# Second layer: the memory's four products by ScalarE with a per-partition scale, in place of two VectorE products

## The reference, cut to what matters

```python
q = x @ Wq.T; k = x @ Wk.T; v = x @ Wv.T            # q: 4 queries x 8 heads x 16, k and v: 8 heads x 16
a_dot   = softmax(q k / 4) v                         # 32 heads of 16
sigma_q = elu(q)                                     # four blocks of 128 features
a_mem   = sigma_q @ memory / (sigma_q @ memory_norm) # one divisor for each token and block
w       = sigmoid(memory_weight)
out     = a_dot * (1 - w) + a_mem * w
```

## Time and profile before

| | |
|---|---|
| median of three runs | 4788.65 us |
| the profiled execution's own time | 4785.47 us |
| its span, first to last instruction | 4783.7 us |
| mean granted TensorE clock | 0.98 of full speed |
| TensorE busy | 4368.3 us (91%) |
| VectorE busy | 3613.1 us (76%) |
| ScalarE busy | 2432.1 us (51%) |
| row maxima on VectorE, L2055, 2048 of them | 1270.6 us busy, 682 ns each |
| exponentials on ScalarE, L1489, 2048 of them | 1090.9 us busy, 602 ns each |
| memory products on VectorE, L2035, 128 of them | 411 to 426 ns each, median 419 |

### The profile page before, as it was taken

How to read it: one execution, slowest core, us unless ns; L and a number is a source line. 1 busy time by engine, 2 the same in 40 slices (tenths; PEclk the granted TensorE clock), 3 DMA queues, 4 the chain that set the end, 5 groups by cost and what they waited for, 6 DMA issues and landing times.

```text
span 4783.7 us, 145033 instructions
## 1 busy us (share of the span) xinstructions
PE 4368.3 (91%) x63104; PEld 3015.0 (63%) x63104; DVE 3613.1 (76%) x7923; ACT 2432.1 (51%) x4881; POOL 708.2 (15%) x909
## 2 busy tenths in 40 slices
PE   6999999999999976999999999999999999999998
PEld 5777777777777765466466466465465465465464
DVE  5777777777777764887877877877877877877876
ACT  4444444444444432744745745745745645645645
POOL 0000000000000001122122122122122122122121
PEclk8999999999999998999999999999999999999999
DMA  3223322233222321000000000000000000000000
GB/s 90 57 74 80 73 66 66 70 76 75 72 66 66 79 65 68 2 19 10 10 19 7 13 19 1 19 19 1 19 19 1 19 19 1 19 19 2 19 10 10
DMA packets 353001, 172.04 MB, mean 36 GB/s; under 512 B 300688, under 2 KB 301584, under 8 KB 351600
## 3 DMA queue, kind: packets, MB, share of 16 engines
q1 hardware_dynamic: 343392, 145.47, 11.4%
q10 hardware_dynamic: 8976, 17.30, 1.3%
HBM read 94.00 MB, written 67.63 MB: 34 GB/s over the span
## 4 chain that ended last, share of the span: by engine, by line
PE 45%; DVE 11%; ACT 2%; issue 1%; POOL 1%; DMA 1%; SPq 0%; DVEq 0%; ACTq 0%; POOLq 0%
PE row_psum L1768 10%; PE row_psum L1793 10%; PE row_psum L40 5%; PE row_psum L42 5%; PE row_psum L41 5%; DVE smax L2055 5%; PE row_psum L1781 4%; PE row_psum L1841 1%; DVE xr_lo L1916 1%; PE row_psum L1821 1%; DVE probs L2035 1%; PE row_psum L1555 1%; DVE stats L1882 1%; POOL rstd L1352 1%; PE row_psum L1740 1%
## 5 line engine op out<-in xcount | busy, mean ns | idle before, releaser
L2055 DVE TENSOR_REDUCE smax<-row_psum 128x1 f32<-128x512 f32 x2048 | 1270.6, 682 | 96.9 <-PE row_psum L1768 96.3
L1489 ACT ACTIVATE probs<-row_psum 128x512 f32<-128x512 f32 x2048 | 1090.9, 602 | 351.6 <-PE row_psum L1781 332.0
L1768 PE MATMUL row_psum<-k_stack,q_stack 64*128 64x512 f32 (+1 forms) x2048 | 740.7, 440 | 50.5 <-DVE smax L2055 24.5
L1781 PE MATMUL row_psum<-q_stack,k_stack 64*128 64x512 f32 (+1 forms) x2048 | 733.4, 458 | 22.6 <-ACT probs L1489 9.0
L1768 PEld LDWEIGHTS row_psum<-k_stack,q_stack 64*128 64x128 f32 (+1 forms) x2048 | 354.2, 188 | 499.7 <-DVE smax L2055 367.9
L1793 PE MATMUL row_psum<-probs,v_aug 128*32 128x512 f32 x4096 | 538.9, 603 | 1.7 <-ACT av_sb L1505 0.4
L1781 PEld LDWEIGHTS row_psum<-q_stack,k_stack 64*128 64x128 f32 (+1 forms) x2048 | 319.1, 184 | 225.3 <-ACT probs L1489 155.4
L939 DVE TENSOR_TENSOR lane_t<-lane_t,lane_p 128x30 f32<-128x30 f32 (+14 forms) x960 | 318.4, 332 | 33.0
L936 DVE TENSOR_TENSOR lane_p<-lane_t 128x30 f32<-128x30 f32 (+14 forms) x960 | 316.4, 330 | 26.5
L40 PE MATMUL row_psum<-wf_hi,xr_hi 128*128 128x320 f32 (+1 forms) x1024 | 332.0, 324 | 4.7 <-DVE xr_lo L1916 3.2
L42 PE MATMUL row_psum<-wf_hi,xr_lo 128*128 128x320 f32 (+1 forms) x1024 | 318.8, 311 | 0.0
(11 more groups left out here) (222 smaller groups left out, 9469.9 us busy)
## 6 DMA issues: line engine op xcount, KB each, us to landing
x_sp<-in_x ACTq DMA_DIRECT2D x33, 512.0 KB, 4.2
tri_dram<-tri SPq DMA_DIRECT2D x256, 64.0 KB, 3.2
lane_t<-tri_dram SPq DMA_DIRECT2D x32, 512.0 KB, 3.9
inv_dram<-lane_t SPq DMA_DIRECT2D x32, 512.0 KB, 2.6
inv_b<-inv_dram SPq DMA_DIRECT2D x256, 64.0 KB, 2.4
x_res<-in_x SPq DMA_DIRECT2D x32, 512.0 KB, 3.9
x<-x_res SPq DMA_DIRECT2D x32, 512.0 KB, 3.1
xs<-x SPq DMA_DIRECT2D x16, 1024.0 KB, 5.5
```

The source lines that it names most:

```text
L1489: act.activation(probs[:, h % PROBS, tt, :], ps[:, m % STACK_BANKS, :], ACT.Exp, scale=float(DH) ** -0.5).then_inc(exp_ready, 1)
L1768: pe.matmul(ps[:, bank, :], q_stack[rows, qt, P * st:P * st + P], k_stack[rows, kv, :], start=True, stop=True).then_inc(max_mm, 1)
L1781: pe.matmul(ps[:, m % STACK_BANKS, :], k_stack[rows, kv, P * tt:P * tt + P], q_stack[rows, qt, :], start=True, stop=True).then_inc(score_m ...
L2055: dve.tensor_reduce(smax[:, g, st:st + 1], ps[:, bank_of("max", NT * g + st), :], AX.X, ALU.max).then_inc(max_ready, 1)
```

## The change

VectorE keeps the reciprocals and their product with `w`. The two products of 128x256 go; in their place ScalarE makes four of 128x128 for each tile, with `ACT.Copy` and a scale that it reads for each partition from `mem_rc`. ScalarE waits for the semaphore that VectorE now raises behind the product with `w` (`mem_consts`, renamed `mem_scales`, counts on from 3), and the last of its four raises `amem_ready`. On ScalarE the four stand in the second half of the same step, behind that half's copies or exponentials, and ahead of the copy into `shift`.

```diff
@@ ScalarE, attention @@
+                def memory(t):
+                    act.wait_ge(mem_scales, 3 + at(b, NT, t + 1))
+                    for n in range(NQ):
+                        c0 = (DKV + 1) * (n % 2)
+                        last = act.activation(a_mem[:, t, DKV * n:DKV * n + DKV], ps[:, 6 + n // 2, c0:c0 + DKV], ACT.Copy,
+                                              scale=mem_rc[:, t, n:n + 1])
+                    last.then_inc(amem_ready, 1)
...
                             act.activation(probs[:, h % PROBS, tt, :], ps[:, m % STACK_BANKS, :], ACT.Exp,
                                            scale=float(DH) ** -0.5).then_inc(exp_ready, 1)
+                        if j == 1 and 0 <= g - MEM_LAG < NT:
+                            memory(g - MEM_LAG)
                         quad, i = divmod(g - MAXT_LAG, 4)
@@ VectorE, attention, memory(t) @@
                     mark(dve.reciprocal(rc, pv[:, :, :, DKV]))
                     dve.wait_ge(dve_own, own[0])
-                    mark(dve.tensor_scalar(rc, rc, mem_w[:, 0:1], None, ALU.mult))
-                    dve.wait_ge(dve_own, own[0])
-                    for c in range(2):
-                        last = dve.tensor_tensor(a_mem[:, t, 2 * DKV * c:2 * DKV * c + 2 * DKV].rearrange("p (n e) -> p n e", n=2),
-                                                 pv[:, c, :, 0:DKV],
-                                                 rc[:, c, :].rearrange("p (n o) -> p n o", o=1).to_broadcast([P, 2, DKV]), ALU.mult)
-                    last.then_inc(amem_ready, 1)
+                    dve.tensor_scalar(rc, rc, mem_w[:, 0:1], None, ALU.mult).then_inc(mem_scales, 1)
```

More of the change, by code:

```diff
@@ L1204, in token_layers @@
         first_in = sem("row_first_in"); w_hi_done = sem("row_w_hi"); w_lo_done = sem("row_w_lo"); c_in = sem("row_c_in")
-        pool_consts = sem("row_pool_consts"); mem_consts = sem("mem_consts")
+        pool_consts = sem("row_pool_consts"); mem_scales = sem("mem_scales")
         x_loaded = [sem("row_x_loaded0"), sem("row_x_loaded1")]
@@ L1430, in begin @@
                 act.wait_ge(c_in, 160)
-                act.activation(mem_w[:, :], mem_w[:, :], ACT.Tanh, scale=0.5).then_inc(mem_consts, 1)
+                act.activation(mem_w[:, :], mem_w[:, :], ACT.Tanh, scale=0.5).then_inc(mem_scales, 1)
                 for t in range(NT):
@@ L1867, in memory_weights @@
             def memory_weights():
[L1868 to L1872, removed]
+                dve.wait_ge(mem_scales, 1)
+                dve.tensor_scalar(mem_wc[:, :], mem_w[:, :], -0.5, 0.5, ALU.mult, ALU.add).then_inc(mem_scales, 1)
+                dve.wait_ge(mem_scales, 2)
+                dve.tensor_scalar(mem_w[:, :], mem_w[:, :], 0.5, 0.5, ALU.mult, ALU.add).then_inc(mem_scales, 1)
+                dve.wait_ge(mem_scales, 3)
             own = [0]
```

## The result

The changed kernel takes 4836.32 us, the median of four runs (4824.68 to 4842.91), where the kernel before takes 4788.0 (4783.44 to 4789.98). The ratio is 1.0101, with a 95% interval of 1.0086 to 1.0116: it is slower by 1%, 48 us. The forecast was 4827, in a range of 4803 to 4851.

What follows compares the result with a forecast made beforehand. The loop from one TensorE memory product to the next would outgrow VectorE's 3.53 us round; 2.02 us at g = 9 plus 0.4 for the shift, times 16 sequences, adds 38.7 us, giving 4827 us, range 4803 to 4851.

Steps and rivals of the forecast that it cites:

- the sign: Whole kernel: slower, chance 0.86; within 0.2%, 0.08; faster by over 0.2%, 0.06.
- the loop: TensorE's memory product through VectorE's row maximum and scales to the next memory product: 3.48 us before, 3.91 after.
- What bounds these steps: Memory steps: TensorE waits for `amem_ready` in 64 places; the loop, formerly hidden under VectorE's 3.53 us, becomes longer than it.
- The four activations, 1.19 us: ScalarE, each tile: four 128x128 activations at 0.38 us with a per-partition scale, overlapping by 0.11, take 1.19 us.
- Along the sequence: Memory products of tiles 1 to 3 late by 0.43, 0.87, 1.24 us; max product of g = 9 by 2.02.
- Busy times: VectorE's busy time falls by 54 us and ScalarE's rises by 97.
- The shift, 0.4 us: Before score 16: the copy into `shift` moves behind the activations, its transfer lands late, adding 0.2 to 0.6, taken as 0.4.
- the sum: 2.02 us at g = 9 plus 0.4 for the shift, 2.4 a sequence, times 16: 38.7 us.
- Nothing later makes it good: Rest of the sequence: VectorE waits for TensorE from 2858.66 on, so the delay is passed on in full.
- the dearer activations: Upper bound: four activations take 1.51 us, losing 3.7 us a sequence, 59 us in all, giving 4848 us.
- Rival A: Step between two memory products: VectorE's relief counts, 0.7 us in 64 places, 45 us faster, 4744 us; chance 0.06.
- Rival C: Harder hit: the operand costs as in L1450 and a full `shift` landing is waited for, 4848 to 4855 us; chance 0.12.

Runs made afterwards that it cites:

- e1_const: The changed kernel with the constant 0.5 as the scale of ScalarE's four activations, in place of the per-partition operand: 4786.66 us, ratio 1.0004 to the kernel before.
- e4_before_exp7: The changed kernel with the last tile's four activations between the exponentials of scores 6 and 7 on ScalarE: 4831.5 us, ratio 1.0096 to the kernel before.
- e8_split: The changed kernel with bank 6 by two activations, bank 7 by one VectorE product, last tile's activations between exponentials of scores 6 and 7: 4789.84 us, ratio 1.0001.
- e6_later: The changed kernel with TensorE's memory product half a step later, between the step's third and fourth max product: 4777.11 us, ratio 0.9976 to the kernel before.
- e7_later_before: The kernel before, its products still on VectorE, with TensorE's memory product between the step's third and fourth max product: 4774.65 us, ratio 0.9974.
- e12_shift_first: e9_bank7 with ScalarE's copy into `shift` ahead of the last tile's four activations: 4767.36 us, ratio 0.9955 to the kernel before.
- e2_half: The changed kernel with only two of the four activations for each tile: 4789.68 us, ratio 1.0006 to the kernel before.
- e3_fill: The changed kernel with TensorE products repeated where it would wait for `amem_ready`: 4818 to 4840 us in three runs, ratio 1.0088 to the kernel before.
- e5_dve_twice: The kernel before with two more products of 128x256 on VectorE for each tile, ahead of its own two: 4852.82 us, ratio 1.0136.
- e9_bank7: e6_later with bank 7 joining the ring of the max products one step later (g = 10): 4788.89 us, ratio 1.0004 to the kernel before.
- e11_fill9: e6_later with six repeats of the next score product in TensorE's wait at g = 9: 4766.05 us, ratio 0.9961 to the kernel before.
- e10_bank7_before: e7_later_before with bank 7 joining the ring of the max products one step later: 4774.65 us, ratio 0.9973 to the kernel before.

## Why the prediction was right

It was right in the sign, in the loop and, within 9 us, in the time; a second mechanism, the clock, was missing, and that the time came so close is partly luck. By its own steps:

- **What bounds these steps: right.** TensorE waited in the same 64 places, longer, and for ScalarE.
- **The four activations, 1.19 us: measured 1.14.** One takes 0.369 us, where 0.38 was built from 0.289 and 0.09 for the operand; `e1_const` puts the operand at 0.085. That is nearer to the rows than to the estimate for all four, 1.27 us, from the figures of the Trainium skill (ScalarE: Activation LUTs, What ACT_TABLE_LOAD costs): by them one takes 0.386 us and two overlap by 0.093, where here one takes 0.369 and they overlap by 0.11.
- **Along the sequence: right, slightly high.** Forecast late by 0.43, 0.87, 1.24 and 2.02 us; measured 0.38, 0.77, 1.14 and 1.90. The 0.05 us too much in the activations enters at each, as the loop says.
- **Busy times: too large.** 44 us less on VectorE and 66 more on ScalarE, for 54 and 97: I had multiplied counts by durations, and instructions of one engine overlap, which busy time does not count twice. Nothing in the sum hung on it. VectorE's waits for max products grew by 6.0 us a sequence (192.6 us for 96.3 in all), for the 4 to 5 forecast.
- **The shift, 0.4 us: too large.** Measured 0.16 at score 16 (2.06 less 1.90). No sequence but one shows a wait for the transfer there. That it was close is right: `e4_before_exp7` and `e8_split` run into it at once.
- **"Nothing later makes it good": not quite.** At full clock the lateness is 2.1 us at the first value product and about 1.55 from one sequence to the next. Where the 0.5 goes I did not settle; the intervals at full clock are few and scatter by 0.4 themselves.
- **The clock: not in the sum.** This is the term that was missing, about +22 us net. The forecast itself had TensorE idle about 1.1 us in each of three tiles and 1.9 us at g = 9, and put the clock at nothing without a reason. No row shown of the kernel before tells at which idle time it falls, so its size could not have been had from them.

So where the sum had 38.7 us, all of it loop, the runs have some 25 of loop and some 22 of clock: errors that partly cancel. The range held because it reached up to the dearer activations, not because it knew of the clock.

Rival A, VectorE's relief, was rightly made unlikely here: VectorE turned idle. But it names something real: once the loop was out of the way, `e6_later` at full clock is about 0.9 us a sequence shorter than `e7_later_before`, which has the same order with the products on VectorE. Rival C did not come: an activation took 0.369 us and not 0.46, nearly every sequence did without a wait for the transfer, and the median stayed under its 4848. What lifted the time above my forecast was the clock, which C did not have.

## What to carry to other kernels

Taking work from the busiest engine pays only if the result comes no later: find who waits for it, add up the way round from that wait to itself, with the hand-over and the operand reads of the new engine, and compare with the round that the busy engine needs. If the loop is the longer one, first move the waiting product to where it has other work ahead of it, then ask whether moving the work still pays. Here the first step alone (`e7_later_before`, 0.9974) gained as much as both together (`e6_later`, 0.9976), and only with the wait at g = 9 shortened as well (`e12_shift_first`, 0.9955) do the moved products look better. And when a wait of TensorE goes, look at every wait of the next few products, their banks' former contents and the transfers too: here `amem_ready`, the copy into `shift` and its transfer stood right behind each other.

## What the runs showed of the hardware that I had not expected

TensorE's clock fell to half (from 2.4 to 1.2 GHz) though TensorE stood idle for no longer than 1.75 us at a time in these steps. The waits of more than 0.25 us from a sequence's first reciprocal to its first value product, and the sequences with a fall there:

| run | TensorE's waits, us | sequences with a fall, of 16 |
|---|---|---|
| before | 0.64, 0.64, 0.64, 0.98 | 0 |
| `e2_half` | 0.51, 0.51, 0.32, 0.51, 1.24 | 4 |
| `e1_const` | 0.67, 0.67, 0.32, 0.67, 1.40 | 7 |
| the change | 1.02, 1.02, 0.32, 1.02, 1.75 | 14 |
| `e3_fill`, the waits filled | 0.44, 0.44, 0.32, 0.45, 0.37 | 2 |
| `e4_before_exp7` | 1.02, 1.02, 0.32, 1.02, 1.34 | 11 |
| `e5_dve_twice` | 1.56, 1.56, 1.56, 1.2 to 1.9 | 16 |
| `e6_later` | 0.32, 1.75 | 12 |
| `e9_bank7` | 0.31, 1.95 | 16 |
| `e11_fill9`, the last wait filled | 0.31, 0.37 | 1 |
| `e12_shift_first` | 0.31, 0.95, 0.52 | 14 |
| `e7_later_before` | 1.24, 1.05, 0.90 | 2 |
| `e10_bank7_before` | 1.24, 1.05, 0.95 | 1 |

In the rows from `e2_half` to the change only the time of the activations differs, and longer waits bring more falls; filling them takes the falls away (`e3_fill`, `e11_fill9`), and the engine that is waited for need not be ScalarE (`e5_dve_twice`). Across different orders the waits do not tell it: `e12_shift_first` has less idle time than the kernel before and falls in 14 sequences, `e7_later_before` has more and falls in 2. So what decides stays open.

A fall of 6.8 us delays the first `av_rc` of a sequence by about 2 us (35.1 for 33.1 behind the first reciprocal, after the change). And falls move: runs with fewer of them behind the memory mostly have more further on (none and 11 of 15 intervals before the change, 14 sequences and 4 intervals after), so their price is to be read from a whole interval and not from the steps alone.
